# Attention's keys: weighted and turned by VectorE in 32x32 blocks and laid out through device memory, in place of the transposes on TensorE

## The chip, the cores and the metric

The kernel runs on one core of one Trainium2 chip. The metric is the device time of one execution in microseconds. A core has TensorE (PE in the profile, with its weight loads as PEld), VectorE (DVE), ScalarE (ACT), GpSimd (POOL) and SyncE (SP), whose queue issues nearly all DMAs of this kernel. Each engine runs its own instructions in order and waits on semaphores for the others.

## What is computed

The reference is a block of four layers on `x` (16 batches, 64 tokens, 512 wide) with a context of the same shape. The change touches the first layer only, grouped-query attention over context and latents, 32 query heads on 8 key heads of 128:

```python
kv = concat([context, layernorm(x)], axis=1)         # 128 keys for each batch
q = rms_norm((layernorm(x) @ Wq) heads) * q_norm_w   # 32 heads
k = rms_norm((kv @ Wk) heads) * k_norm_w             # 8 heads
v = (kv @ Wv) heads
scores = einsum('bhgqd,bhkd->bhgqk', q, k) / sqrt(128)
x = x + (softmax(scores) @ v) heads @ Wo
```

Behind it come a feed-forward layer with weights quantized to 4 bits, an attention without projections, and a feed-forward layer with low-rank parts. All is in float32; the large products are made as three products of high and low parts.

## The kernel before

Attention is cut into 64 units: key head g (8 of them) by pair of batches p (8). `run_steps` runs `*_step0` for each step j on every engine, and a unit passes through the stages with a lag: in step j the kernel projects queries and keys of unit j, makes the scores of unit j-1, the softmax of unit j-2, the product with the values of unit j-3 and the output projection of unit j-4. `st.has(lag, UNITS)` says whether a stage has a unit in this step.

PE's order in a full step is written out in `pe_step0`: the query projection (L439, 12 products of 512 columns), the key and value projection (L459, 24 of 256), the two key transposes of unit j-1 (L485), the output projection of unit j-4 (L505, 12 of 512), the values (L526), the scores of unit j-1 (L469). In step 3 the scores of unit 2 come right behind the transposes, ahead of the values.

The queries already go another way than the keys. DVE scales them (L711) from PSUM bank `b_q` into bank `b_n`, in an order in which each 32x32 block can be turned by itself, and turns the blocks (L717) into `qB`. SP writes `qB` to `q_turn` in device memory (`blocks_out`, L372) and reads it back as `qT` (`blocks_back`, L376). The probabilities take the same way (L691, L696, `p_turn`, `pR`). The read of unit j's queries waits until the scores of unit j-1 are done, since `qT` is a single buffer.

The keys: ACT sums their squares (L632, squares into `ksq`), DVE makes the mean (L720), POOL the power -0.5 (L808), DVE the scaled keys `kn` (L723), PE two transposes into bank 2 (L485), ACT a copy to `kT` that multiplies by the product of both norm weights (L626, one number for each partition, `wqk[:, 3:4]`). DVE then adds the output projection into `acc` (L740), and its next step begins with the row maximum of the scores (L674) and the low part of the values (L678), for which the key projection two units later waits (`s_vlo`).

SP's queue in `sp_step0`: probabilities out, weight pieces, stores of dequantized weights, queries out, probabilities back, loads for the dequantization, queries back. In step 0 the loads of the last quantization table and of four index lists (`sp_tables(sp, (2,))`, `sp_indices`, L887 to L902) stand behind the queries' read.

## Time and profile before

| what | value |
|---|---|
| median of 3 runs | 1081.14 us (1079.81 to 1081.6) |
| the profiled execution | 1080.24 us, span 1078.4 us |
| PE busy | 1038.6 us (96%) |
| DVE busy | 711.7 us (66%) |
| ACT busy | 536.8 us (50%) |
| POOL busy | 469.5 us (44%) |
| mean granted TensorE clock | 0.995 of full speed |
| attention's steps | to about 700 us of the span |

Busy time is the time in which an engine executes; matmuls overlap in the pipeline, so starts tell more than durations. The span is what the profile covers; the run's own time is 1.8 us longer.

### The profile page before, as it was taken

The numbers are of one execution on the slowest core, as the hardware profiler recorded it, in microseconds if no ns is written. First come the engines' busy times: TensorE is split into PE (matmuls) and PEld (weight loads), VectorE is DVE, ScalarE is ACT, GpSimd is POOL, SyncE is SP. The second block draws the span as 40 slices with busy tenths as digits, with TensorE's granted clock in tenths as the row PEclk, the third lists the DMA queues.
The fourth block names the chain that finished last, engine by engine and source line by source line (L and its number), as shares of the span: only waits on it lengthen the run. The fifth ranks groups of instructions, "written<-read, shape, count | busy, mean of one in ns | idle before, by whom it ended". The sixth has DMA issues, their size and how long they took to land. (4 is left out here: it accounts for less than half of the span.)

```text
span 1078.4 us, 18680 instructions
## 1 busy us (share of the span) xinstructions
PE 1038.6 (96%) x6021; PEld 897.1 (83%) x6021; DVE 711.7 (66%) x1435; ACT 536.8 (50%) x1974; POOL 469.5 (44%) x446
## 2 busy tenths in 40 slices
PE   5899999999999999999999999899999999899998
PEld 5789999999899899899999998778777877677877
DVE  6677767667666667667676666653345666889862
ACT  3555555555555555555555454433324445456531
POOL 3445454565554554554645433300013325566521
PEclk9999999999999999999999999999999999899999
DMA  8447766676667666766666435242021344233301
GB/s 284 112 130 226 207 192 198 195 206 196 199 198 195 201 192 186 214 204 201 210 191 187 145 99 167 98 136 82 1 59 40 79 108 108 69 69 69 89 11 40
DMA packets 151397, 156.18 MB, mean 145 GB/s; under 512 B 19640, under 2 KB 104656, under 8 KB 151300
## 3 DMA queue, kind: packets, MB, share of 16 engines
q1 hardware_dynamic: 146804, 138.08, 44.0%
q0 software_dynamic: 4496, 16.91, 5.3%
q8 instruction: 49, 0.80, 0.3%
q14 instruction: 48, 0.39, 0.1%
HBM read 98.19 MB, written 44.30 MB: 132 GB/s over the span
## 5 line engine op out<-in xcount | busy, mean ns | idle before, releaser
L459 PEld LDWEIGHTS bank<-wqkv,kvT 128*128 128x128 f32 x1536 | 193.9, 193 | 8.2 <-issue 3.6
L439 PE MATMUL bank<-wqkv,kvT 128*128 128x512 f32 x768 | 195.4, 404 | 5.0 <-DVE wqkv L746 2.5
L459 PE MATMUL bank<-wqkv,kvT 128*128 128x256 f32 x1536 | 196.2, 285 | 3.0 <-issue 3.0
L800 POOL TENSOR_TENSOR rms<-msq,half_neg 128x4 f32<-128x4 f32 x64 | 79.5, 1242 | 270.0 <-DVE msq L703 270.0
L505 PE MATMUL bank<-wo,aoT 128*128 128x512 f32 x768 | 190.7, 398 | 0.3 <-DVE aoT L659 0.3
L439 PEld LDWEIGHTS bank<-wqkv,kvT 128*128 128x128 f32 x768 | 141.2, 191 | 34.1 <-issue 3.2
L505 PEld LDWEIGHTS bank<-wo,aoT 128*128 128x128 f32 x768 | 139.8, 189 | 26.4 <-DVE aoT L659 0.5
L606 ACT ACTIVATE prob<-bank,nmax 128x128 f32<-128x128 f32 x256 | 90.4, 365 | 56.4 <-DVE nmax L674 56.4
L646 ACT ACTIVATE aoT<-bank 128x512 fp32r<-128x512 f32 x64 | 38.2, 597 | 121.7 <-PE bank L526 96.2
L803 POOL TENSOR_TENSOR pT<-pR,pT 128x512 fp32r<-128x512 f32 x64 | 82.3, 1286 | 14.4 <-ACT pT L595 14.4
L613 ACT ACTIVATE qB<-bank 128x128 f32<-128x128 f32 x256 | 67.3, 278 | 39.7 <-PE bank L439 36.2
L711 DVE TENSOR_TENSOR bank<-bank,rms 128x512 f32<-128x512 f32 x64 | 44.8, 699 | 55.8 <-POOL rms L800 55.8
L1054 PE MATMUL bank<-x2T,wgu 128*128 128x512 f32 (+1 forms) x336 | 80.9, 396 | 0.4 <-DVE wgu L1015 0.4
L2125 POOL TENSOR_TENSOR pr<-pr,rc 128x512 f32<-128x512 f32 x52 | 54.4, 1048 | 54.5 <-DVE rc L1989 54.3
L674 DVE TENSOR_REDUCE nmax<-bank 128x4 f32<-128x512 f32 x64 | 44.2, 691 | 50.1 <-PE bank L469 50.0
L1054 PEld LDWEIGHTS bank<-x2T,wgu 128*128 128x128 f32 (+1 forms) x336 | 62.4, 187 | 15.9 <-DVE wgu L1015 0.8
L626 ACT ACTIVATE kT<-bank,wqk 128x256 f32<-128x256 f32 x64 | 30.6, 478 | 87.9 <-PE bank L485 87.9
L469 PE MATMUL bank<-kT,qT 128*128 128x128 f32 x512 | 67.8, 275 | 2.0 <-DMA qT<-q_turn 1.3
L1073 PE MATMUL bank<-wd,hT 128*128 128x512 f32 (+1 forms) x264 | 65.5, 396 | 0.0
L469 PEld LDWEIGHTS bank<-kT,qT 128*128 128x128 f32 x512 | 62.8, 192 | 2.5 <-DMA qT<-q_turn 1.5
L723 DVE TENSOR_TENSOR kn<-bank,rms 128x256 f32<-128x256 f32 x64 | 27.2, 425 | 52.0 <-POOL rms L808 52.0
L1869 ACT ACTIVATE pmT<-bank 128x512 fp32r<-128x512 f32 x64 | 38.2, 596 | 46.4 <-PE bank L1588 46.2
(176 smaller groups left out, 2021.4 us busy)
## 6 DMA issues: line engine op xcount, KB each, us to landing
q_turn<-qB SPq DMA_DIRECT2D x64, 256.0 KB
qT<-q_turn SPq DMA_DIRECT2D x64, 256.0 KB, 3.6
p_turn<-pB SPq DMA_DIRECT2D x64, 256.0 KB, 2.1
pR<-p_turn SPq DMA_DIRECT2D x64, 256.0 KB
qS<-qhl SPq DMA_DIRECT2D x32, 256.0 KB, 3.7
wqkv_raw<-in_L_xattn_Wq_dram SPq DMA_DIRECT2D x30, 256.0 KB
wo_raw<-in_L_xattn_Wo_dram SPq DMA_DIRECT2D x30, 256.0 KB
wload<-w_gu SPq DMA_DIRECT2D x20, 256.0 KB, 3.2
```

The lines of the kernel that those rows point to most:

```text
L439: mm = pe.matmul(b_q[:, :], kvT[:, l, kt, p, 1:3, :], wqkv[:, par, r, kt, 0:QW], start=(kt == 0 and n == 0), stop=(kt == KT - 1 and n == 2))
L459: mm = pe.matmul(kv_bank(st, 0)[:, b * 256:(b + 1) * 256], kvT[:, l, kt, p, 2 * b:2 * b + 2, :], wqkv[:, par, r, kt, QW:QKV], start=(kt == ...
L469: mm = pe.matmul(b_s[:, n * P:(n + 1) * P], qT[:, n, :, :], kT[:, n // 2, :], start=True, stop=True)
L505: mm = pe.matmul(b_o[:, :], aoT[:, l, h, :, :], wo[:, par, r, h, :], start=(h == 0 and n == 0), stop=(h == G - 1 and n == 2))
L606: act.activation(prob[:, :, n, :], b_s[:, n * P:(n + 1) * P].rearrange("p (k b) -> p b k", b=4), ACT.Exp, bias=nmax[:, n:n + 1], accum_out ...
L613: act.activation(qB[:, h, :, :], b_q[:, h * HD:(h + 1) * HD], ACT.Square, accum_out=ssq[:, h:h + 1]).then_inc(s_qsq, 1)
L711: dve.tensor_tensor(b_n[:, :].rearrange("p (b h d) -> p b h d", b=4, h=G), b_q[:, :].rearrange("p (h d b) -> p b h d", h=G, b=4), rms[:, 0 ...
L800: pool.tensor_tensor(rms[:, 0:4], msq[:, 0:4], half_neg[:, 0:4], ALU.pow).then_inc(s_rq, 1)
L803: pool.tensor_tensor(pT[:, LO, :, :, :], pR[:, :, :, :], pT[:, HI, :, :, :].bitcast(F32), ALU.subtract).then_inc(s_plo, 1)
L1054: mm = pe.matmul(b[0:w, :], wgu[:, f, l, m, kt, 0:w], x2T[:, r, kt, :], start=(kt == 0 and k == 0), stop=(kt == KT - 1 and k == 2))
L1073: mm = pe.matmul(f_d[t][:, :], hT[0:w, l, t * P:(t + 1) * P], wd[0:w, f, r, :], start=(f == 0 and k == 0), stop=(f == FT - 1 and k == 2))
L2125: pool.tensor_tensor(of[:, to + t % KT, :], of[:, to + t % KT, :], rc1[:, t % 4:t % 4 + 1].to_broadcast([P, D]), ALU.mult).then_inc(s_n1, 1)
```

## The change

The keys take the queries' way. DVE multiplies the keys of each batch by their norm factor and by the norm weights (now a row of 128 numbers on every partition, loaded with a broadcast) in one `scalar_tensor_tensor` for each of the two batches, from the projection's bank into `b_n`, turns the blocks into `kB`, and SP writes `kB` to `k_turn` and reads it back as `kT`. PE's two transposes and ACT's copy are gone, and `kn` and `ksq` with them: ACT writes the squares into bank 2 (`b_sq`). The cut diff:

```diff
-        kn = sb("kn", [P, 2, HD], F32, s0b)
+        kB = sb("kB", [P, G, 2, 32], F32, s0b)
-        kT = sb("kT", [P, 2, P], F32, s0b)
+        kT = sb("kT", [P, G, 2, 32], F32, s0b)
+        wqk = sb("wqk", [P, 2, HD], F32, s0b)
...
+        k_turn = nc.dram_tensor("k_turn", (G, P, 2 * 32), F32).ap()
...
-            sp.dma_start(wqk[:, 0:1], a["L0_xattn_q_norm_w"].rearrange("(d o) -> d o", o=1)).then_inc(s_nw, 16)
+            sp.dma_start(wqk[:, 0, :], a["L0_xattn_q_norm_w"].rearrange("(o d) -> o d", o=1)
+                         .to_broadcast([P, HD])).then_inc(s_nw, 16)
...
             def sp_step0(st):
+                if st.has(1, UNITS):
+                    sp.wait_ge(s_k_out, st.done(1, 16))
+                    wait(sp, s_s, st.done(2))
+                    blocks_back(sp, kT[:, :, :, :], k_turn).then_inc(s_k_back, 16)
                 if st.has(2, UNITS):
...
                 sp_loads(sp, st.j)
                 if st.has(0, UNITS):
+                    sp.wait_ge(s_kB, st.done(0))
+                    wait(sp, s_k_back, st.done(1, 16))
+                    blocks_out(sp, k_turn, kB[:, :, :, :]).then_inc(s_k_out, 16)
                     sp.wait_ge(s_q_out, st.done(0, 16))
                     wait(sp, s_s, st.done(1))
                     blocks_back(sp, qT[:, :, :, :], q_turn).then_inc(s_q_back, 16)
...
-            pe.wait_ge(s_kT, st.done(1))
+            pe.wait_ge(s_k_back, st.done(1, 16))
...
-                mm = pe.matmul(b_s[:, n * P:(n + 1) * P], qT[:, n, :, :], kT[:, n // 2, :], start=True, stop=True)
+                mm = pe.matmul(b_s[:, n * P:(n + 1) * P], qT[:, n, :, :], kT[:, :, n // 2, :], start=True, stop=True)
...
-            if st.has(1, UNITS):
-                pe.wait_ge(s_kn, st.done(1))
-                wait(pe, s_kT, st.done(2))
-                for b in range(2):
-                    mm = pe.transpose(turn_bank(st)[:, b * P:(b + 1) * P], kn[:, b, :], ident[:, :])
-                mm.then_inc(s_tk, 1)
...
-                act.activation(kT[:, :, :], turn_bank(st)[:, 0:256].rearrange("p (b k) -> p b k", b=2), ACT.Copy,
-                               scale=wqk[:, 3:4]).then_inc(s_kT, 1)
...
-                    act.activation(ksq[:, b, :], by_key(kv_bank(st, 0))[:, b, 0:HD], ACT.Square,
+                    act.activation(b_sq[:, b * HD:(b + 1) * HD], by_key(kv_bank(st, 0))[:, b, 0:HD], ACT.Square,
...
                 dve.wait_ge(s_rk, st.done(0))
-                wait(dve, s_tk, st.done(1))
-                dve.tensor_tensor(kn[:, :, :], by_key(kv_bank(st, 0))[:, :, 0:HD],
-                                  rms[:, 4:6].unsqueeze(2).to_broadcast([P, 2, HD]), ALU.mult).then_inc(s_kn, 1)
+                if st.j == 0:
+                    dve.wait_ge(s_idx_n, 2)
+                for b in range(2):
+                    mul = dve.scalar_tensor_tensor(
+                        out=b_n[:, 0:256].rearrange("p (a b d) -> p b a d", a=4, b=2)[:, b, :, :],
+                        in0=by_key(kv_bank(st, 0))[:, b, 0:HD].rearrange("p (d a) -> p a d", a=4),
+                        scalar=rms[:, 4 + b:5 + b], in1=wqk[:, 1, :].rearrange("p (d a) -> p a d", a=4),
+                        op0=ALU.mult, op1=ALU.mult)
+                mul.then_inc(s_kn, 1)
+                dve.wait_ge(s_kn, st.done(0))
+                wait(dve, s_k_out, st.done(1, 16))
+                dve.transpose(kB[:, :, :, :].rearrange("p a b t -> p (a b t)"), b_n[:, 0:256]).then_inc(s_kB, 1)
...
-            dve.tensor_tensor(wqk[:, 2:3], wqk[:, 0:1], wqk[:, 1:2], ALU.mult).then_inc(s_idx_n, 1)
+            dve.tensor_tensor(wqk[:, 0, :], wqk[:, 0, :], wqk[:, 1, :], ALU.mult).then_inc(s_idx_n, 1)
```

## Rows read from the trace of the kernel before

**Rows 1.** The page's busy time of each engine over the whole span.

```profile
PE 1038.6 (96%) x6021; PEld 897.1 (83%) x6021; DVE 711.7 (66%) x1435; ACT 536.8 (50%) x1974; POOL 469.5 (44%) x446
```

**Rows 2.** Windows: stretch, length, PE PEld DVE ACT POOL busy us, clock, DMA share, GB/s.

```profile
40.00:60.00 20.00, 14.73 (x95) 12.65 (x95) 16.76 (x40) 11.30 (x49) 9.36 (x10) 0.99 0.44 138
...
300.00:500.00 200.00, 200.00 (x1251) 180.44 (x1250) 137.23 (x275) 110.92 (x490) 107.34 (x92) 1.00 0.68 201
```

**Rows 3.** Timeline of PE, one attention step (start us, duration us, engine, line).

```profile
303.58 3.01 PE L439 MATMUL bank<-wqkv,kvT 128*128 128x512 f32 x12
...
306.43 3.04 PE L459 MATMUL bank<-wqkv,kvT 128*128 128x256 f32 x24
...
309.30 0.38 PE L485 MATMUL bank<-ident,kn 128*128 128x128 f32 x2
...
309.44 2.98 PE L505 MATMUL bank<-wo,aoT 128*128 128x512 f32 x12
...
312.25 0.88 PE L526 MATMUL bank<-pT,vv 128*128 128x256 f32 x6
...
312.97 1.06 PE L469 MATMUL bank<-kT,qT 128*128 128x128 f32 x8
...
313.78 3.01 PE L439 MATMUL bank<-wqkv,kvT 128*128 128x512 f32 x12
```

**Rows 4.** Timeline of DVE around the turn of one attention step.

```profile
301.53 0.42 DVE L723 TENSOR_TENSOR kn<-bank,rms 128x256 f32<-128x256 f32 x1 [0.81 <-POOL rms L808]
...
302.26 0.69 DVE L740 TENSOR_TENSOR acc<-bank,acc 128x512 f32<-128x512 f32 x1 [0.30 <-PE bank L505]
...
303.86 0.69 DVE L674 TENSOR_REDUCE nmax<-bank 128x4 f32<-128x512 f32 x1 [0.91 <-PE bank L469]
...
304.47 0.41 DVE L678 TENSOR_TENSOR vv<-bank,vv 128x256 fp32r<-128x256 f32 x1
```

**Rows 5.** Groups by line and shape, 20 to 830 us: xcount, busy us, mean ns.

```profile
L717 DVE STREAM_TRANSPOSE qB<-bank 128x512 f32<-128x512 f32 x64 | 45.9, 717 | 2.2
...
L711 DVE TENSOR_TENSOR bank<-bank,rms 128x512 f32<-128x512 f32 x64 | 44.8, 699 | 55.8 <-POOL rms L800 55.8
...
L485 PE MATMUL bank<-ident,kn 128*128 128x128 f32 x128 | 24.4, 273 | 0.0
...
L1274 DVE SCALAR_TENSOR_TENSOR gact<-gact,bank 128x512 f32<-128x512 f32 x5 | 3.4, 687 | 5.9 <-ACT gact L1166 5.9
```

**Rows 6.** The page's DMA queue (packets, MB, share) and one issue group (us to landing).

```profile
q1 hardware_dynamic: 146804, 138.08, 44.0%
...
p_turn<-pB SPq DMA_DIRECT2D x64, 256.0 KB, 2.1
```

**Rows 7.** Timeline of SP's DMA issues in start-up, steps 0 and 1.

```profile
28.54 0.39 SPq L376 DMA_DIRECT2D qT<-q_turn  x1
...
31.97 0.64 SPq L902 DMA_DIRECT2D idx_raw<-in_L_ffn_down_g_idx_dram  x1
...
33.20 0.35 SPq L372 DMA_DIRECT2D q_turn<-qB  x1
...
36.45 0.38 SPq L376 DMA_DIRECT2D qT<-q_turn  x1
```

**Rows 8.** Timeline of PE in start-up: first scores, then key projections of units 2 to 4.

```profile
31.33 1.16 PE L469 MATMUL bank<-kT,qT 128*128 128x128 f32 x8 [1.26 <-DMA qT<-q_turn]
...
35.87 3.11 PE L459 MATMUL bank<-wqkv,kvT 128*128 128x256 f32 x24 [0.61 <-issue]
...
47.41 3.11 PE L459 MATMUL bank<-wqkv,kvT 128*128 128x256 f32 x24 [2.37 <-issue]
...
59.14 4.61 PE L459 MATMUL bank<-wqkv,kvT 128*128 128x256 f32 x24
```

**Rows 9.** Windows view: one microsecond of start-up, columns as in rows 2.

```profile
61.00:62.00 1.00, 1.00 (x6) 1.00 (x6) 1.00 (x2) 0.74 (x2) 0.96 (x1) 0.50 0.22 80
```

**Rows 10.** Timeline of DVE in start-up: the maximum of unit 1's scores.

```profile
46.28 0.69 DVE L674 TENSOR_REDUCE nmax<-bank 128x4 f32<-128x512 f32 x1
```

More of the change, by code:

```diff
@@ L107, in block_kernel @@
         rstd = sb("rstd", [P, 4, PAIRS], F32)
-        wqk = sb("wqk", [P, 4], F32)
         s0 = ExitStack()
@@ L125, in block_kernel @@
         qB = sb("qB", [P, G, G, 32], F32, s0b)
-        ksq = sb("ksq", [P, 2, HD], F32, s0b)
         pB = sb("pB", [P, G, G, 32], F32, s0b)
-        kn = sb("kn", [P, 2, HD], F32, s0b)
+        kB = sb("kB", [P, G, 2, 32], F32, s0b)
         qT = sb("qT", [P, G, G, 32], F32, s0b)
-        kT = sb("kT", [P, 2, P], F32, s0b)
+        kT = sb("kT", [P, G, 2, 32], F32, s0b)
         vv = sb("vv", [P, 2, 2, 2, HD], F32R, s0b)
+        wqk = sb("wqk", [P, 2, HD], F32, s0b)
         prob = sb("prob", [P, 4, 4, 32], F32, s0b)
@@ L236, in block_kernel @@
         s_q, s_kv, s_s, s_pv, s_o = (sem(f"s_{n}") for n in ("q", "kv", "s", "pv", "o"))
-        s_qsq, s_ksq, s_kT, s_vhi, s_exp, s_phi, s_aohi = (
-            sem(f"s_{n}") for n in ("qsq", "ksq", "kT", "vhi", "exp", "phi", "aohi"))
+        s_qsq, s_ksq, s_vhi, s_exp, s_phi, s_aohi = (
+            sem(f"s_{n}") for n in ("qsq", "ksq", "vhi", "exp", "phi", "aohi"))
         s_qms, s_kms, s_qn, s_kn, s_vlo, s_max, s_plo, s_pn, s_aolo, s_acc = (
             sem(f"s_{n}") for n in ("qms", "kms", "qn", "kn", "vlo", "max", "plo", "pn", "aolo", "acc"))
-        s_qB, s_tk, s_pB = sem("s_qB"), sem("s_tk"), sem("s_pB")
-        s_q_out, s_p_out = sem("s_q_out"), sem("s_p_out")
-        s_q_back, s_p_back = sem("s_q_back"), sem("s_p_back")
+        s_qB, s_kB, s_pB = sem("s_qB"), sem("s_kB"), sem("s_pB")
+        s_q_out, s_k_out, s_p_out = sem("s_q_out"), sem("s_k_out"), sem("s_p_out")
+        s_q_back, s_k_back, s_p_back = sem("s_q_back"), sem("s_k_back"), sem("s_p_back")
         s_rq, s_rk = sem("s_rq"), sem("s_rk")
@@ L247, in block_kernel @@
         b_kv = (bank[3], bank[1])
-        b_n = bank[5]
+        b_sq, b_n = bank[2], bank[5]
+        k_turn = nc.dram_tensor("k_turn", (G, P, 2 * 32), F32).ap()
         q_turn = nc.dram_tensor("q_turn", (G, P, P), F32).ap()
@@ L252, in block_kernel @@
         STEPS0 = UNITS + 4
-        def turn_bank(st):
-            return bank[2] if st.j < UNITS else b_q
         def unit(st, lag):
@@ L325, in sp_first @@
             context(2)
-            sp.dma_start(wqk[:, 0:1], a["L0_xattn_q_norm_w"].rearrange("(d o) -> d o", o=1)).then_inc(s_nw, 16)
-            sp.dma_start(wqk[:, 1:2], a["L0_xattn_k_norm_w"].rearrange("(d o) -> d o", o=1)).then_inc(s_nw, 16)
+            sp.dma_start(wqk[:, 0, :], a["L0_xattn_q_norm_w"].rearrange("(o d) -> o d", o=1)
+                         .to_broadcast([P, HD])).then_inc(s_nw, 16)
+            sp.dma_start(wqk[:, 1, :], a["L0_xattn_k_norm_w"].rearrange("(o d) -> o d", o=1)
+                         .to_broadcast([P, HD])).then_inc(s_nw, 16)
             latents(3)
@@ L621, in act_step0 @@
                 x2_hi(act, 1)
-            if st.has(1, UNITS):
-                act.wait_ge(s_tk, st.done(1))
-                if st.j == 1:
-                    act.wait_ge(s_idx_n, 2)
-                act.activation(kT[:, :, :], turn_bank(st)[:, 0:256].rearrange("p (b k) -> p b k", b=2), ACT.Copy,
-                               scale=wqk[:, 3:4]).then_inc(s_kT, 1)
             if st.has(0, UNITS):
@@ L758, in dve_first @@
             dve.wait_ge(s_nw, 32)
-            dve.tensor_tensor(wqk[:, 2:3], wqk[:, 0:1], wqk[:, 1:2], ALU.mult).then_inc(s_idx_n, 1)
+            dve.tensor_tensor(wqk[:, 0, :], wqk[:, 0, :], wqk[:, 1, :], ALU.mult).then_inc(s_idx_n, 1)
             dve.wait_ge(s_idx_n, 1)
-            dve.tensor_scalar(wqk[:, 3:4], wqk[:, 2:3], float(HD) ** -0.5, None, ALU.mult).then_inc(s_idx_n, 1)
+            dve.tensor_scalar(wqk[:, 1, :], wqk[:, 0, :], float(HD) ** -0.5, None, ALU.mult).then_inc(s_idx_n, 1)
             dve_statistics(dve, 2)
```

## The prediction

> **What bounds the kernel now.** I read the page's busy times first: PE works 96% of the span, DVE 66% [rows 1]. Then the windows by stretch: from 300 to 500 us PE is busy for all 200 us, in start-up (40 to 60 us) for only 14.73 of 20, and there DVE is busy for 16.76 [rows 2]. So two regimes stand side by side: a steady one that PE sets, from about 60 us to 671 us, and a start-up that something else sets. PE's timeline shows the steady step as a closed ring: query projection at 303.58, key projection 306.43, transposes 309.30, output projection 309.44, values 312.25, scores 312.97, the next query projection 313.78, with no idle time noted anywhere [rows 3]. The period is 10.20 us. What DVE does in that step is the other thing to see: it waits 0.30 us for the output projection before L740 and 0.91 us for the scores before L674 [rows 4]. DVE is late for nobody and has 1.2 us of rest in a step at this point.
>
> **The change, part by part.** *The transposes on PE.* A record of L485 lasts 273 ns [rows 5], but that is pipeline depth. What a pair costs is start to start: from 309.30 to 309.44, 0.14 us [rows 3]. The queue of PE is full, so the slot is given back if nothing new makes PE wait. Bounds: 0.10 us, if the first product of L505 needs a little more room right behind L459; 0.19 us, if half of the pair's record of 0.38 us [rows 3] stood clear of its neighbours. I take 0.14, as the starts are what the period is made of. Steps 4 to 63 are ones in which PE is the bound or becomes it: 60 x 0.14 = 8.4 us (6.0 to 11.4).
>
> *ACT's copy.* One ACT instruction of a step goes; ACT is half idle, and the only reader of its time here is the sum of squares, which DVE reads behind its own transpose L717. Nothing gained, nothing lost; the squares' new home in PSUM costs ACT nothing that anyone waits for.
>
> *DVE.* Out goes L723, 0.42 us [rows 4]. In come two multiplies of 128 elements and one block transpose of 256. From 512 elements at 0.69 us (L740) and 256 at 0.42 [rows 4] one element costs 1.05 ns and the fixed part is 0.15 us, so 128 elements take 0.29 us; the form with two operations costs what the plain one does (L1274, 687 ns for 512), and reading every fourth element does not either (L711, 699 ns) [rows 5]. A transpose of 512 takes 717 [rows 5], so one of 256 some 0.45. Neighbours on DVE overlap by about 0.08 us (303.86 + 0.69 against a start at 304.47 [rows 4]), which gives 0.21 + 0.29 + 0.45 + 0.03 for the wait between them = 0.98 us, 0.56 more than before; bounds 0.45 and 0.90 (each multiply as dear as the one of 256). Where does it go? L723 ends at 301.95; the new work would end at 302.51, L740 starts 0.25 us late and ends at 303.20, and the scores are there at 303.86, or 303.72 with the shorter step. So 0.5 us of the rest remain, the addition is covered. Even uncovered, the next cover is at L459: the low part of the values is done at 304.88, and PE asks for it at 306.43, 1.55 us later [rows 3, 4].
>
> *SP and DMA in the steady step.* SP gets two waits and two issues. The write of unit j is queued behind the loads and ahead of the queries' read, which waits for the scores (303.86) anyway; `kB` is there at 302.5, so SP waits no longer than before. The read heads the next step: it waits for the write's landing (2.1 us, as `p_turn` [rows 6]), so it is issued at about 305 and lands 2.8 to 3.6 us later, at 309; the scores come at 312.97 [rows 3]. Cover: 4 us. The probabilities' write queued behind it is ready at 307.8 only. The bytes: 128 packets of 1 KB and 512 of 256 B in a step. All packets of the queue took 44% of 16 engines' time for 146804 of them [rows 6], 52 ns each; 640 more are 2.1 us on each of 16 engines in a step, and the DMA share of 0.68 [rows 2] goes to at most 0.88. That costs latency, which the 4 us cover.
>
> The Trainium skill (DMA: Bandwidth & Descriptors, section "Why small descriptors are slow") puts the overhead of a packet of 256 bytes at 27%. No row here splits a packet's time, so nothing can be said for or against it; by that figure the 512 small packets would be the dearest part of the addition, inside the ceiling of 0.88 above.
>
> *Start-up.* Here is the price. In step 0 SP issues the queries' read at 28.54, then the last table and four index lists until 32.61, and only then step 1 begins [rows 7]. The keys' read is now the first entry of step 1, behind all of them. PE waited until 31.33 for `qT` [rows 8], 2.8 us after its issue. The keys' read, issued at 32.65, lands at 35.5 by that, or at 35.9 by the 3.2 us that the write of 33.20 took behind the index lists (the next read goes at 36.45, as it waits for that landing) [rows 7]. I take 35.9: unit 0's scores come 4.6 us late, after almost 6 us of idle PE. What a rest does to the clock: 24 products of the key projection take 3.11 us at 35.87 and 47.41, and 4.61 us at 59.14, behind two rests of some 2 us each; the granted clock there was 0.50 of full speed, the level of 1.2 GHz [rows 8, 9]. So behind the longer rest I expect the half clock, +0.8 us on the scores and about 1.5 us on the query projection behind it. DVE then takes unit 0's maximum at 37.6 in place of 34.75 (it was busy with other work until then), +2.9. The query projection of unit 2 ends 2 us later still than that order gives, of which 1.3 us reaches DVE through the squares; the key work of unit 2 adds 0.56. So unit 1's maximum, at 46.28 before [rows 10], comes at 51.0. From there to unit 4's key projection (59.14 [rows 8]) DVE is the bound (16.76 of 20 us busy [rows 2]) and adds the 0.56 of unit 3: +5.3 us in all, rounded to 5.2. The keys' reads of units 1 and 2 come in time by this order (unit 2's lands at 53.5, its scores start at 54.9). Bounds: 2.4 us, with a landing after 2.5 us, no fall of the clock and 1.1 us of DVE; 8.3 us, with a landing 0.7 us later and the fall of 1.5 us paid once more.
>
> The norm weights as rows make two DVE operations of 128 elements out of two of one (0.29 against the fixed 0.15 us each), ahead of step 0; DVE waits for unit 0's queries behind them, so that covers them, and without the cover it is 0.3 us.
>
> *The end.* In step 64 there is no projection, and PE waits for DVE's work on the next layer while unit 63's queries land; the keys' read follows theirs within 0.4 us. No cost. The layers behind attention are untouched.
>
> *Sum.* The profiled execution took 1078.4 us and 1.8 around it. 1080.2 - 8.4 + 5.2 = 1077.0. The median of the runs lies 0.9 above the profiled one, so 1077.9.
>
> **The rivals.** *A cheap start.* If the half clock does not set in, or its fall at 59 us goes away, start-up costs 2.4: 1081.1 - 8.4 + 2.4 = 1075.1. For it: the clock stayed full behind the rest of 2.37 us at 47.41 [rows 8]. Against: the new rest is more than twice as long. Chance 0.18.
>
> *A dear start.* 8.3 us: 1081.0, no change. For it: the index lists are in the queue ahead of the read, and every later step of start-up has a rest too. Chance 0.14.
>
> *DVE becomes the bound (the slower side).* DVE's ring is 10.20 - 0.91 - 0.30 = 8.99 us now; with 0.56 it is 9.55 against PE's 10.06. It decides from an addition of 1.07 us on. If reads that are strided on both inputs, or `b_n` used three times in a step with waits between, bring it to 1.3, the period is 8.99 + 1.3 = 10.29 and the time 1081.1 + 60 x 0.09 + 5.2 = 1091.7. For it: three more passes each step on the engine that sets start-up. Against: the rows show neither surcharge [rows 5]. Chance 0.07.
>
> The Trainium skill (VectorE: DVE Perf Modes, section "Rules for kernel authors") speaks against this change: it gives a 128x128 transpose to TensorE where the result may lie in PSUM, and to VectorE only blocks of 32x32. The trace so far disagrees for this kernel, since the pair costs the full engine 0.14 us and the exchange costs 0.56 us on the one with rest; by the rule the time would be that of this rival.
>
> *The slot is not given back.* Nothing gained, start-up paid: 1081.1 + 5.2 = 1086.3. For it: only that ends of matmuls are modelled. Against: the starts add up to the period. Chance 0.05.
>
> *The keys' read comes late each step.* DMA share near 0.9 and landings over 7 us; each us beyond the cover is 60 us. Chance 0.02, for 1100 and more.
>
> **How the numbers follow.** The forecast, 1077.9, has 0.54; its own range is 1076.0 to 1079.5. The range over all, with no more than 2 in 10 left out, is 1073.5 to 1083.5. A measurement of this kernel can tell about 0.2% (2.2 us) from no change, so faster means below 1079.0: 0.18 from the cheap start and 0.42 of the forecast, 0.60. Within 0.2%: 0.12 of the forecast and 0.11 of the dear start, 0.23. Slower: the rest, 0.17.
>
> **What would show it.** In PE's timeline of after: L505 at 0.02 us or less where L485 stood, and a period of 10.06 us (right) or 10.2 (slot or DVE). No idle before the scores in steady steps. DVE's wait for the scores at 0.3 to 0.5 us. In start-up: the first scores at 36 us with an idle of 6 us released by the DMA `kT`, the granted clock at half behind it, unit 1's maximum at 51 us. I am wrong if the keys' read lands elsewhere in SP's queue, or if steady steps show a wait for `kT` or for `vv`.

## The result

The change makes the kernel slower: 1094.76 us (median of 4 runs, 1091.59 to 1099.81) against 1080.47 for the kernel before on the same chips; ratio 1.0131, 95% interval 1.0108 to 1.0154. The forecast was 1077.9, the range ended at 1083.5. The profiled execution took 1094.41 us with a span of 1092.6, 14.2 more than the span of before.

The first look is at the busy times, and at the windows of start-up and of the steady part (columns as in [rows 2]), of the changed kernel:

```profile
PE 1031.1 (94%) x5893; PEld 882.9 (81%) x5893; DVE 757.4 (69%) x1563; ACT 514.8 (47%) x1910; POOL 470.3 (43%) x446
```

```profile
40.00:60.00 20.00, 17.05 (x112) 15.27 (x111) 14.63 (x36) 10.68 (x46) 8.82 (x9) 0.95 0.45 137
300.00:500.00 200.00, 195.74 (x1203) 173.93 (x1202) 149.26 (x310) 103.17 (x473) 103.95 (x89) 1.00 0.76 220
```

Against [rows 1]: PE is busy for 7.5 us less, VectorE for 45.7 more. Against [rows 2]: PE was busy for all of 300 to 500 us and now rests 4.3 us of them. VectorE, with 149 us of 200, is not full. Something new makes PE wait in the steady part.

PE's timeline of after shows a step that nothing disturbs, and further on one that is disturbed (columns as in [rows 3]; a bracket is the idle time before the instruction):

```profile
308.05 1.06 PE L476 MATMUL bank<-kT,qT 128*128 128x128 f32 x8
308.86 3.01 PE L446 MATMUL bank<-wqkv,kvT 128*128 128x512 f32 x12
311.71 3.04 PE L466 MATMUL bank<-wqkv,kvT 128*128 128x256 f32 x24
314.58 2.91 PE L506 MATMUL bank<-wo,aoT 128*128 128x512 f32 x12
317.33 0.88 PE L527 MATMUL bank<-pT,vv 128*128 128x256 f32 x6
...
324.57 2.91 PE L506 MATMUL bank<-wo,aoT 128*128 128x512 f32 x12
...
548.26 1.13 PE L476 MATMUL bank<-kT,qT 128*128 128x128 f32 x8 [1.94 <-issue]
```

The output projection starts at 314.58 and 324.57: a period of 9.99 us in place of 10.20 [rows 3]. So the slot of the transposes is given back, and it was worth 0.21 us, not 0.14. The gain is eaten by other steps. Setting the start of the output projection of each step beside that of the kernel before gives this account of the two spans (+ is later):

| stretch | us |
|---|---|
| start-up, to step 4 | +3.65 |
| 59 steps by 0.205 from step 4 to step 63 | -12.1 |
| step 6, stalled | +2.9 |
| steps 7 to 62, stalls in 20 of them, the longest 2.2 us | +15.6 |
| steps 64 and 65, where the next layer sets in | +3.2 |
| later | +1.0 |
| sum | +14.2 |

The account sets one execution beside one other. Executions of kernels whose code is the same there differ by up to some 3 us in start-up and by some 2 us in steps 64 and 65 (shown below), so the first and the last rows are less certain than the steady ones.

The stalls of the steady part are the item to explain. What SP waited for between 80 and 640 us of after (engine and line, what for, us in total, times, longest):

```profile
SPq L383 <- DMA k_turn<-kB: 153.7, 53, 7.1
SPq L918 <- DMA w_gu<-qch: 41.4, 24, 2.4
...
SPq L379 <- DVE pB L691: 7.8, 7, 2.9
```

and of before:

```profile
SPq L372 <- DVE pB L696: 172.8, 55, 3.6
...
SPq L914 <- DMA w_gu<-qch: 13.9, 19, 2.2
```

Before, SP stood at the head of each step waiting for the probabilities: it was early. Now it stands there waiting for the keys' write to land, and the probabilities stand ready behind it. SP's own timeline in after has the whole ring:

```profile
304.98 0.37 SPq L383 DMA_DIRECT2D kT<-k_turn  x1
305.47 0.43 SPq L379 DMA_DIRECT2D p_turn<-pB  x1
...
307.59 0.41 SPq L930 DMA_DIRECT2D w_gu<-qch  x1
...
311.42 0.56 SPq L918 DMA_DIRECT2D qch<-in_L_ffn_up_qweight_dram  x1
312.06 0.54 SPq L379 DMA_DIRECT2D k_turn<-kB  x1
312.70 0.39 SPq L383 DMA_DIRECT2D qT<-q_turn  x1
314.96 0.37 SPq L383 DMA_DIRECT2D kT<-k_turn  x1
315.43 0.46 SPq L379 DMA_DIRECT2D p_turn<-pB  x1
```

and VectorE's timeline of after beside it says when the data of these transfers were ready:

```profile
308.28 0.45 DVE L728 STREAM_TRANSPOSE kB<-bank 128x256 f32<-128x256 f32 x1
...
309.23 0.67 DVE L669 TENSOR_REDUCE nmax<-bank 128x4 f32<-128x512 f32 x1
...
312.43 0.72 DVE L691 STREAM_TRANSPOSE pB<-bank 128x512 f32<-128x512 f32 x1
...
318.41 0.80 DVE L720 SCALAR_TENSOR_TENSOR bank<-bank,rms,wqk 128x128 f32<-128x128 f32 x2 [0.81 <-POOL rms L812]
319.24 0.45 DVE L728 STREAM_TRANSPOSE kB<-bank 128x256 f32<-128x256 f32 x1
```

The keys' read goes out at 304.98, the probabilities' write behind it at 305.47, then the store of dequantized weights (307.59); the load at 311.42 waits for that store's landing; the keys' write stands behind the load and goes out at 312.06, 3.3 us after `kB` was complete (308.73); and the next keys' read (314.96) stands behind the write's landing. `pB` was complete at 313.15 and goes out at 315.43, 2.3 us late. All that SP waits for in this round are landings of its own transfers, and from read to read it takes 9.98 us, as long as PE's step, so nothing is left over. That equality belongs to this round only: the stores and loads differ from step to step, and the twelve rounds whose read goes out between 294 and 409 us last 8.81 to 12.77 us. What tells most is how long the probabilities lie ready before their write goes out, in the median of the steps between 95 and 640 us: 0.03 us in the kernel before, 2.2 us here. A store or a write that lands late then moves what is behind it: the probabilities reach PE late (L527 waits 7.8 us in 10 steps between 80 and 640 us), or the keys seem to (L476, 4.6 us in 9 steps, such as the 1.94 us above; the profile names no releaser there, but the keys' read had gone out at 545.94 only, 2.3 us before the scores).

Start-up is the other item. SP, after:

```profile
29.01 0.38 SPq L383 DMA_DIRECT2D qT<-q_turn  x1
...
32.42 0.64 SPq L906 DMA_DIRECT2D idx_raw<-in_L_ffn_down_g_idx_dram  x1
33.10 0.43 SPq L383 DMA_DIRECT2D kT<-k_turn  x1
```

and PE, after:

```profile
36.09 2.05 PE L476 MATMUL bank<-kT,qT 128*128 128x128 f32 x8 [6.54 <-DMA kT<-k_turn]
37.78 4.89 PE L446 MATMUL bank<-wqkv,kvT 128*128 128x512 f32 x12
```

The read behind the index lists, PE idle for 6.5 us, the scores and the query projection at half speed (2.05 us against 1.06, 4.89 against 3.01; the granted clock of 36 to 41 us was 0.50 of full speed, the level of 1.2 GHz): that is what was forecast.

### The profile page after: what moved, and what is told of

Read it like the earlier page. It is cut to its first block and busy times, and to the rows that moved or that the text cites. A ratio compares the mean times of both kernels' runs of the same rounds, so it can differ in the third digit from the quotient of the medians.

```text
span 1092.6 us, 18679 instructions
## 1 busy us (share of the span) xinstructions
PE 1031.1 (94%) x5893; PEld 882.9 (81%) x5893; DVE 757.4 (69%) x1563; ACT 514.8 (47%) x1910; POOL 470.3 (43%) x446
## 5 line engine op out<-in xcount | busy, mean ns | idle before, releaser
L506 PE MATMUL bank<-wo,aoT 128*128 128x512 f32 x768 | 186.4, 391 | 1.4 <-DVE aoT L654 1.4
L506 PEld LDWEIGHTS bank<-wo,aoT 128*128 128x128 f32 x768 | 140.3, 188 | 28.2 <-DVE aoT L654 1.5
L720 DVE SCALAR_TENSOR_TENSOR bank<-bank,rms,wqk 128x128 f32<-128x128 f32 x128 | 51.1, 446 | 52.1 <-POOL rms L812 52.1
L476 PE MATMUL bank<-kT,qT 128*128 128x128 f32 x512 | 69.9, 280 | 11.1 <-DMA kT<-k_turn 6.5
L476 PEld LDWEIGHTS bank<-kT,qT 128*128 128x128 f32 x512 | 64.1, 195 | 13.1 <-issue 12.3
L527 PEld LDWEIGHTS bank<-pT,vv 128*128 128x128 f32 x384 | 53.3, 190 | 19.3 <-POOL pT L807 15.4
L527 PE MATMUL bank<-pT,vv 128*128 128x256 f32 x384 | 57.6, 286 | 9.5 <-POOL pT L807 9.2
L1873 ACT ACTIVATE pmT<-bank 128x512 fp32r<-128x512 f32 x64 | 38.2, 597 | 46.1 <-PE bank L1592 45.7
```

The source lines that it names most:

```text
L476: mm = pe.matmul(b_s[:, n * P:(n + 1) * P], qT[:, n, :, :], kT[:, :, n // 2, :], start=True, stop=True)
L506: mm = pe.matmul(b_o[:, :], aoT[:, l, h, :, :], wo[:, par, r, h, :], start=(h == 0 and n == 0), stop=(h == G - 1 and n == 2))
L527: mm = pe.matmul(b_pv[:, b * 256:(b + 1) * 256], vv[:, par, l, b, :], pT[:, r, :, b, :], start=(n == 0), stop=(n == 2))
```

## Experiments: each part alone, on the kernel before

The theory after the result: the wait at the head of SP's queue costs the time; traffic, VectorE's work and the missing transposes do not. Rivals: the DMA engines are overloaded by 640 more packets in a step, or VectorE's longer chain delays PE.

**No transposes.** The kernel before without the two transposes; ACT copies `kn`, and the keys enter the scores unturned.

```diff
-                for b in range(2):
-                    mm = pe.transpose(turn_bank(st)[:, b * P:(b + 1) * P], kn[:, b, :], ident[:, :])
-                mm.then_inc(s_tk, 1)
...
-                act.activation(kT[:, :, :], turn_bank(st)[:, 0:256].rearrange("p (b k) -> p b k", b=2), ACT.Copy,
+                act.activation(kT[:, :, :], kn[:, :, :], ACT.Copy,
```

> The kernel before without the two key transposes on PE, and with nothing in their place: ACT copies the keys from kn without turning them, so the scores are not the reference's. It measures the slot alone. In the undisturbed steps of the changed kernel the period is 9.99 us against 10.20, so 0.21 us a step and not the 0.14 of the forecast: 60 x 0.21 = 12.6 us, 1068 us. If the forecast's 0.14 were right and the rest of the 0.21 came from elsewhere (ACT, the other order), 1072 us. If the slot were not given back, 1080.

Measured: 1070.24 us, ratio 0.990 (0.9881 to 0.992). The period is 9.99 us, so the slot is 0.21 us, and the whole of it is worth 9.6 us. It is less than 60 x 0.21 because of places where PE does not set the pace: step 6 takes 13.0 us here, against 10.20 in the kernel before, and the last steps take 1.5 us more; start-up came 1.5 us earlier in this execution. In step 6 VectorE of this kernel waits for the first load of quantized weights:

```profile
83.84 0.49 DVE L1205 TENSOR_SCALAR qch<-qch,shift 128x512 int32<-128x512 int32 x1 [4.58 <-DMA qch<-_L_ffn_gate_qweight_dram]
```

No keys travel in this kernel, so that stall does not need them.

**The traffic alone.** The kernel before, and in each step a write of 128 KB from `kvT` to a spare array and a read of it back in the same shapes as the keys' (of the edit only the read is shown). The read waits for the write of the step before last, which has long landed.

```diff
+                if st.has(2, UNITS):
+                    sp.wait_ge(s_k_out, st.done(2, 16))
+                    wait(sp, s_k_back, st.done(3, 16))
+                    blocks_back(sp, kY[:, :, :, :], k_turn[st.j % 2]).then_inc(s_k_back, 16)
```

> The kernel before with the added DMA traffic alone: at the changed kernel's places in SP's queue 128 KB is written to device memory and 128 KB read back in each step, from and to tiles that nobody waits for, through two buffers, so that the read at the head of a step waits for the write of the step before last. The squares lie in PSUM to make room. Theory Q (SP's queue: the read at the head of a step waits for the landing of the write issued just before, and holds the probabilities' write and all behind it): no wait, so at most 2 us more than before, 1080 to 1083. Rival C (contention: more packets make every landing later): the 18.7 us of stalls return, 1095 or more. In either case the landings tell by how much traffic alone lengthens them.

Measured: 1081.07 us, ratio 1.0004 (0.9992 to 1.0016). Window of 300 to 500 us:

```profile
300.00:500.00 200.00, 200.00 (x1254) 180.37 (x1253) 137.36 (x274) 111.81 (x488) 108.39 (x93) 1.00 0.77 225
```

The DMA share is 0.77, as in after (0.76), PE does not rest, and the probabilities' write still goes out 0.03 us after its data are ready. Overload falls as the cause.

**The same traffic, and the wait.** One thing differs from the kernel above: the read at the head of the step waits for the write of the step just before.

```diff
-                if st.has(2, UNITS):
-                    sp.wait_ge(s_k_out, st.done(2, 16))
-                    wait(sp, s_k_back, st.done(3, 16))
-                    blocks_back(sp, kY[:, :, :, :], k_turn[st.j % 2]).then_inc(s_k_back, 16)
+                if st.has(1, UNITS):
+                    sp.wait_ge(s_k_out, st.done(1, 16))
+                    wait(sp, s_k_back, st.done(2, 16))
+                    blocks_back(sp, kY[:, :, :, :], k_turn[(st.j - 1) % 2]).then_inc(s_k_back, 16)
```

> The kernel before with the same unused traffic as b2_traffic and one difference: the read at the head of a step waits for the landing of the write issued in the step just before it, as in the changed kernel. PE, DVE and ACT have the old work. Theory Q (the wait at the head of SP's queue is enough to cause the steady stalls): 1090 or more. If the stalls need the key data itself (PE waiting for kT) or the added DVE work, 1080 to 1083 as b2_traffic.

Measured: 1089.23 us, ratio 1.0072 (1.0046 to 1.0098). Its window and what SP waited for:

```profile
300.00:500.00 200.00, 195.23 (x1218) 174.48 (x1217) 135.71 (x266) 108.11 (x475) 103.00 (x89) 1.00 0.75 218
```

```profile
SPq L389 <- DMA k_turn<-kvT: 147.0, 53, 5.3
```

PE rests 4.8 us in this stretch, as in after (4.3), though no result of these transfers is used by anyone. The profiled execution collects 8.9 us of stalls in steps 7 to 62. They can only come through what is queued behind the wait on SP. The probabilities lie ready for 2.2 us in the median, as in after. This is the clearest of the runs: by the two ratios the wait by itself costs about 7 us, the bytes nothing that can be told from zero. It makes 8.9 of the 15.6 us of stalls of after. The others come only where PE also needs the keys and VectorE has the new work; no run parts these two, but the next section shows that nearly all of them go when the read changes its place.

**VectorE's work.** The kernel before, and the two multiplies once more on VectorE, into the bank `b_n`.

```diff
+                for b in range(2):
+                    mul = dve.scalar_tensor_tensor(
+                        out=b_n[:, 0:256].rearrange("p (a b d) -> p b a d", a=4, b=2)[:, b, :, :],
+                        in0=by_key(kv_bank(st, 0))[:, b, 0:HD].rearrange("p (d a) -> p a d", a=4),
+                        scalar=rms[:, 4 + b:5 + b], in1=ident[:, :].rearrange("p (d a) -> p a d", a=4),
+                        op0=ALU.mult, op1=ALU.mult)
```

> The kernel before with the two new multiplies of DVE added behind the scaling of the keys (0.80 us a step, as much as the change adds to DVE in all, 0.86), their result unused. Theory Q: the steady steps cover it, start-up pays two or three times 0.8, so 1080.5 + 0 to 2.5. Rival D (DVE becomes the bound in the steady steps): 1090 or more.

Measured: 1082.46 us, ratio 1.0019 (1.0008 to 1.0029). In the profiled execution steps 7 to 63 gain and lose nothing; step 4 starts 1.0 us later, step 6 takes 0.3 us more and the last steps 2.3. So 0.8 us more of VectorE in each step is covered in the steady part, as forecast. That the multiplies are what costs the rest is not shown: the last steps take 2.0 us more with the traffic alone, too, where VectorE has no new work.

Two further looks say what a multiply costs. With both inputs read plainly, and then with only the one in SBUF read plainly and the one in PSUM in steps of four as before:

> b3_dve_multiplies with both inputs of the added multiplies read in plain order (elements next to each other), the output still in blocks of 32; for the duration of one multiply alone. If the stride of the inputs is what makes it 443 ns in place of the 290 of the forecast, about 290; if it is the operation with a number for each partition and a second tensor, 440 still.

> b3_dve_multiplies with the weights alone (the input in SBUF) read in plain order, the keys from PSUM still every fourth element. If the stride in SBUF costs the time, about 290 ns; if the stride in PSUM does, 440.

The group of L728 in the three kernels, in this order (group, busy us and mean ns of one, idle before):

```profile
L728 DVE SCALAR_TENSOR_TENSOR bank<-bank,rms,ident 128x128 f32<-128x128 f32 x128 | 50.8, 443 | 0.0
```

```profile
L728 DVE SCALAR_TENSOR_TENSOR bank<-bank,rms,ident 128x128 f32<-128x128 f32 x128 | 39.0, 350 | 0.0
```

```profile
L728 DVE SCALAR_TENSOR_TENSOR bank<-bank,rms,ident 128x128 f32<-128x128 f32 x128 | 38.9, 350 | 0.0
```

One execution each (1083.5 and 1081.36 us) tells nothing of the whole time, but the groups are clear: 93 ns of the 443 are the strided read from SBUF, the strided read from PSUM is free, and the form itself takes 350, not the 290 that I had worked out.

## Experiments: moves in SP's queue, on the changed kernel

**The keys' read behind the probabilities' write.** The same instructions, one of them elsewhere:

```diff
             def sp_step0(st):
-                if st.has(1, UNITS):
-                    sp.wait_ge(s_k_out, st.done(1, 16))
-                    wait(sp, s_s, st.done(2))
-                    blocks_back(sp, kT[:, :, :, :], k_turn).then_inc(s_k_back, 16)
                 if st.has(2, UNITS):
...
                     blocks_out(sp, p_turn, pB[:, :, :, :]).then_inc(s_p_out, 16)
+                if st.has(1, UNITS):
+                    sp.wait_ge(s_k_out, st.done(1, 16))
+                    wait(sp, s_s, st.done(2))
+                    blocks_back(sp, kT[:, :, :, :], k_turn).then_inc(s_k_back, 16)
```

> The changed kernel with one move in SP's order: the keys' read stands behind the probabilities' write and no longer ahead of it. Theory Q: the probabilities' write goes when it is ready, the waits of PE for their low part (9.2 us) and of ACT for the probabilities go; what remains is held back with the rest of the queue, so 1084 to 1090. Rivals C and D: no change, 1093 to 1097.

Measured: 1082.6 us, ratio 1.0027 (1.001 to 1.0043): 11.5 of the 14.3 us above the kernel before are gone, more than expected. PE is busy for all 200 us from 300 to 500 again, the stalls of steps 7 to 62 fall from 15.6 to 1.7 us, and SP is early again:

```profile
SPq L379 <- DVE pB L691: 127.5, 49, 3.5
...
SPq L383 <- DMA k_turn<-kB: 25.2, 23, 2.5
```

The read still waits for its write, but 23 times and behind the probabilities, and SP's rest before them (3.5 us at most) takes up what a late store costs. The probabilities' write goes out 0.03 us after its data are ready, as in the kernel before, although the rounds from read to read still last 8.0 to 12.1 us: what counts is what is queued behind the wait.

**The keys' write ahead of the loads.** The read stays at the head.

```diff
-                sp_loads(sp, st.j)
                 if st.has(0, UNITS):
...
                     blocks_out(sp, k_turn, kB[:, :, :, :]).then_inc(s_k_out, 16)
+                sp_loads(sp, st.j)
+                if st.has(0, UNITS):
```

> The changed kernel with the other move alone: the keys' write stands ahead of the dequantization's load (which waits for a store to land) and no longer behind it; the read stays at the head of the step. Theory Q: the write goes when the keys are ready, 2 to 3 us earlier in two steps of three, so its landing is over by the time the probabilities are ready and most steady stalls go: 1083 to 1088. If the stalls come from the read's place alone, no change: 1093 to 1097.

Measured: 1084.95 us, ratio 1.0032 (1.0011 to 1.0052). Stalls of 2.3 us are left in steps 7 to 62. So either cut opens the ring: the landing of the store is the link that this one takes out, and the probabilities' write is what the other frees. But step 6 now takes 6.9 us beyond its 9.99.

**The last table and the index lists behind unit 0's keys' read**, in step 1 in place of step 0, the steady order as in after:

```diff
                     blocks_back(sp, kT[:, :, :, :], k_turn).then_inc(s_k_back, 16)
+                if st.j == 1:
+                    sp_tables(sp, (2,))
+                    sp_indices(sp)
...
-                if st.j == 0:
-                    sp_tables(sp, (2,))
-                    sp_indices(sp)
```

> The changed kernel with the last table and the four index lists issued behind unit 0's keys' read, in step 1. In the profile of the changed kernel PE waited 6.5 us for that read and its clock fell behind it. Theory: the read is issued at 29.4 and lands at 32.5, so 3 us less at the first output projection, 1091 to 1092; the steady stalls stay.

Measured: 1088.1 us, ratio 1.0084 (1.0051 to 1.0117). Step 4 starts 0.95 us later than before in place of 3.65, so by this pair the lists cost 2.7 us of start-up. The other profiled executions agree in direction: the four kernels with the lists ahead of the keys' read start step 4 3.65 to 4.8 us later than the kernel before, the five with the lists behind it from 0.8 us earlier to 2.7 us later. The steady stalls remain (14.1 us), and step 6 hardly stalls (0.3 us beyond 9.99). The time is some 3 us below what was expected.

**Moves together.** First all three, where the lists stand at the head of step 1 and so still ahead of the keys' read; then the read and the lists, with the lists really behind the read; then all three with the lists behind.

> The changed kernel with all three moves in SP's order: the keys' read behind the probabilities' write, the keys' write ahead of the dequantization's load, the tables behind unit 0's keys' read. Theory Q: 60 steps of 9.99 us, start-up 1 to 2 us late by DVE's added work (b3_dve_multiplies lost 1.3 us by the first output projections and 2.3 us in steps 64 and 65), the end 2 to 3.5 us late: 1079.8 - 12.4 + 1.5 + 3 = 1072 (1070 to 1075), faster than both kernels.

> The changed kernel with two moves in SP's order: the keys' read behind the probabilities' write, and the last table and the index lists behind unit 0's keys' read (in a4_all they stood ahead of it after all, in step 1). Theory: a1_read_behind_p lost 4.3 us by the first output projection and 4.3 in step 6 (there DVE waits for the first dequantization loads, which the late start pushes back); with the lists behind, 1.0 and 0.3 as a3_tables_behind. Steady 59 x 0.21 = 12.4 saved less 2 us of single stalls, 3.5 us lost in steps 64 and 65: 1080 + 1.3 - 10.4 + 3.5 = 1074.5 (1072 to 1077). If step 6 is a matter of the read's place and not of the start, 1078 or more.

> As a5_read_and_tables, and the keys' write ahead of the dequantization's load. Theory: no single stalls in the steady steps (none in a4_all from step 8 to 62), but the first loads of step 5 go up to 1 us later: 1072 to 1076. If the write ahead of the loads is what made step 6 of a4_all so dear (9.2 us), 1078 or more.

| moves | us | ratio, 95% | to step 4 | step 6 | stalls 7 to 62 |
|---|---|---|---|---|---|
| none (after) | 1094.76 | 1.0131 (1.0108 to 1.0154) | +3.65 | +2.9 | 15.6 |
| read | 1082.6 | 1.0027 (1.001 to 1.0043) | +4.3 | +4.5 | 1.7 |
| write | 1084.95 | 1.0032 (1.0011 to 1.0052) | +4.6 | +6.9 | 2.3 |
| lists | 1088.1 | 1.0084 (1.0051 to 1.0117) | +0.95 | +0.3 | 14.1 |
| all, lists ahead of the read | 1085.39 | 1.0032 (1.0012 to 1.0052) | +4.8 | +9.4 | 0 |
| read, lists | 1078.57 | 0.9989 (0.9972 to 1.0007) | +0.9 | +4.0 | 1.5 |
| all, lists behind the read | 1080.25 | 0.9994 (0.998 to 1.0008) | -0.3 | +7.8 | 0 |

(Step 6: what it takes beyond 9.99 us; to step 4: against the kernel before; both in the profiled execution.) All three kernels came out slower than expected, by 4 to 13 us. With all three moves the steady stalls are gone entirely, but what was won there is lost in step 6. I had written that a late start-up pushes step 6 into trouble. The last row refutes it: no late start, and +7.8.

What holds step 6 shows on VectorE, in the kernel with read and lists moved:

```profile
84.02 0.83 DVE L1215 TENSOR_SCALAR qch<-qch,shift 128x512 int32<-128x512 int32 x1 [2.35 <-DMA qch<-_L_ffn_gate_qweight_dram]
...
87.70 1.71 DVE L1219 TENSOR_TENSOR qch<-qch,rows 128x512 f32<-128x512 int32 x1 [1.22 <-DMA rows<-table_gate,idx]
```

and on PE:

```profile
91.25 1.33 PE L476 MATMUL bank<-kT,qT 128*128 128x128 f32 x8 [1.36 <-DMA qT<-q_turn]
```

VectorE's rows are the first two pieces of the dequantization, whose loads SP issues at 80.16, right behind the seven table copies and among the exchanges of queries, keys and probabilities; the DMA share between 80 and 85 us is 0.89, from 85 to 90 it is 1.00. The rest of VectorE's work for attention stands behind these two waits. PE rests as well, but not by that way alone: its longest rest in step 6 of this trace, 1.36 us, stands before the scores, which need both reads. The queries' read, which the profile names, went out at 82.18 and had landed at 90.29; the keys' read went out at 88.01 only, when the keys' write of 81.55 had landed after 6.4 us. So the long landings of the exchange itself hold PE here too. The query projection behind it takes 4.49 us in place of 3.01.

**The two loads and the table copies earlier; weights in plain order.** Three kernels: the weights' row stored in the order in which the multiplies take it; with it the two loads and the seven copies of step 5 issued at the end of step 4; and this last move on the kernel before. (The copies and the two loads leave their places in step 5; those deletions are not shown.) The first two stand on top of the read and the lists moved.

```diff
-                        scalar=rms[:, 4 + b:5 + b], in1=wqk[:, 1, :].rearrange("p (d a) -> p a d", a=4),
+                        scalar=rms[:, 4 + b:5 + b], in1=wqk[:, 1, :].rearrange("p (a d) -> p a d", a=4),
...
-            dve.tensor_scalar(wqk[:, 1, :], wqk[:, 0, :], float(HD) ** -0.5, None, ALU.mult).then_inc(s_idx_n, 1)
+            dve.tensor_scalar(wqk[:, 1, :].rearrange("p (a d) -> p a d", a=4),
+                              wqk[:, 0, :].rearrange("p (d a) -> p a d", a=4), float(HD) ** -0.5, None, ALU.mult).then_inc(s_idx_n, 1)
```

```diff
                     blocks_back(sp, qT[:, :, :, :], q_turn).then_inc(s_q_back, 16)
+                if st.j == 4:
+                    quantized_load(sp, 0)
+                    quantized_load(sp, 1)
+                    for k, (m, n, g) in enumerate(WEIGHTS):
+                        for b in range(-(-n // D)):
+                            w = min(D, n - b * D)
+                            sp.dma_start(table[k, b][:, 0:w], z_line[k][:, b * D:b * D + w]).then_inc(s_tab, 16)
```

> The kernel with the keys' read behind the probabilities' write and the last tables behind unit 0's keys' read (1078.6, 0.9989 of the kernel before); in addition the norm weights stand in the row in the order in which the multiplies take them, so that the operand in SBUF is read plainly. Theory (PE sets the steady step, DVE only start-up, step 6 and the last steps): each multiply takes 350 ns in place of 443, the steady period stays at 9.99 us, and the time falls by 0.3 to 0.9 us, 1077.9. Rival (DVE sets the time somewhere in steady steps after all): 60 x 0.19 us less, 1067.

> The kernel of c1_plain, and the first two dequantization loads and the seven table copies of step 5 issued at the end of step 4, where SP rests 3.5 us and the DMA share is 0.3 to 0.4. Theory (step 6 stalls since these loads and the exchanges of queries, keys and probabilities meet in a full queue at 80 to 90 us): VectorE's two waits there (2.35 and 1.22 us) go, the stall of 3.75 us at step 7 falls below 1 us, the clock stays full, and the time is 1074.5 (0.995 of before). Rival (the stall comes from the longer work of VectorE there, or the table copies now hold the probabilities' write of step 5): the stall stays at 3 to 4 us, 1078.

> The kernel before with that same move of loads and copies from step 5 to the end of step 4, and nothing else. It shows what the move is worth without the change. Theory: in the kernel before, VectorE's waits at step 6 (0.96 and 0.52 us) do not reach PE (steps there are 10.2 us), so nothing is gained, 1080.5 within 1 us. Rival (it gains as much there as in c2_early): 1077.

Measured: plain order 1074.87 us, ratio 0.9941 (0.9916 to 0.9966); with the early loads 1075.04, ratio 0.9934 (0.9907 to 0.9962); the early loads on the kernel before 1080.01, ratio 0.9994 (0.9977 to 1.0011). With the early loads VectorE has no wait for a load or a gather between 76 and 100 us, step 6 takes 9.99 us, and the clock is full there:

```profile
80.00:90.00 10.00, 10.00 (x63) 8.99 (x62) 6.97 (x15) 5.42 (x24) 6.42 (x7) 1.00 0.88 259
```

against the plain order alone:

```profile
80.00:90.00 10.00, 8.02 (x50) 6.80 (x49) 5.56 (x12) 4.56 (x20) 5.59 (x6) 1.00 0.95 287
```

So with those first loads and gathers early, the stall of step 6 is gone, as expected. This is one execution of each kernel, and loads and copies were moved together; the changed kernel with the lists alone moved lost only 0.3 us in step 6 with the loads in their old place. The lateness of the loads is therefore the likely cause, not one shown beyond doubt. The kernel before had the same meeting with slack to spare, so there the move is worth nothing. What the medians do not show is a gain of the early loads over the plain order (1074.87 against 1075.04, the runs of each spread over 5 to 6 us), although step 6 takes 2.5 us less in the profiled execution. Why stays open: the start-up of the profiled executions differs by 3.4 us (-0.76 and +2.66 us to step 4) although the two kernels are the same up to there, and the plain order's profiled execution, 1078.86, was the slowest of its six. For the same reasons I leave open how much of the 3.7 us between 1078.57 and 1074.87 is the plain order's (it was sized at 0.3 to 0.9, the two stand on different chips, and each multiply did fall to 354 ns). The steady period stayed at 9.99 us, so VectorE does not set it.

Both of these are faster than the kernel before, by 0.6%. The change has something to give; as it stood, the place of one instruction in SP's queue cost it 11.5 us (14.3 us above the kernel before on its chips, against 2.8).

## Why the prediction was wrong, point by point

- **The slot.** Mechanism right: given back, closed ring, bound PE. The term was mis-sized: 0.21 us, not 0.14 (bounds 0.10 to 0.19), 12.1 us and not 8.4. I took the distance of two starts, L485 to L505 [rows 3]; the rest of the pair's price lay behind it: from L505 to L526 it was 2.81 us [rows 3], from L506 to L527 it is 2.75. What shows the price is the period with and without.
- **VectorE.** The block transpose took 0.45 us as forecast, each multiply 446 ns and not 290. From the first start to the last end the new work takes 1.28 us in place of 0.42 (307.45 to 308.73 in the step above), so the addition is 0.86 us and not 0.56, within the upper bound of 0.90. Covered in the steady part, as said; 1.07 us, the point from which this rival decides, was not reached, and its expected sign (a period of 10.29 us) did not come: the loss has another cause. The rule of the Trainium skill that gives whole transposes to TensorE (VectorE: DVE Perf Modes, section "Rules for kernel authors") would have steered clear of this loss, but not for its reason: with the keys' read behind the probabilities' write, the lists moved and the weights in plain order the version without TensorE's transposes is the faster one, by 0.6% (1074.87 us, ratio 0.9941).
- **SP and DMA in the steady step: this is the step that failed.** It said "`kB` is there at 302.5, so SP waits no longer than before", "it waits for the write's landing (2.1 us, as `p_turn`)" and "the probabilities' write queued behind it is ready at 307.8 only". The landing of `k_turn` took 4.5 us in the median (the traffic alone: 3.3), more than twice the row that I had taken. The write did not go out when `kB` was ready but behind a load that waits for a store's landing, which in turn was issued behind the read at the head. I looked at each wait with the others held still; they form a ring through SP, and its sum, 9.98 us in the round shown and up to 12.77 in others, is what had to be set against PE's 9.99. And the cover that I counted, 4 us until the scores, is the keys' own. What stood behind the read, the probabilities' write, had its own deadline, and no cover was worked out for it beyond its being later: it went out a median 2.2 us late, PE waited, and the steady steps lost 15.6 us that the sum put at nothing.
- **Its rival.** "The keys' read comes late each step" had 0.02 and a price of over 1100. It came nearest, but came in 20 steps of 56, not in all, and through the ring, not through the DMA share: 0.76, below the 0.88 allowed for, and at 0.77 harmless in the kernel with the traffic alone.
- **Start-up.** Right in mechanism and near in size: read issued at 33.10 (32.65), scores at 36.09 (35.9), idle 6.54 us (almost 6), half clock on the scores and the query projection, unit 1's maximum at 51.56 (51.0). It came to 3.65 us at step 4 in place of 5.2, in one execution, and with the lists moved 2.7 of them go.
- **Step 6.** Not seen. [rows 2] start their steady stretch at 300 us, and I took steps 4 to 63 as PE's from there. The row that would have told is VectorE's wait for the first load in the kernel before, 0.96 us at 82.04: a place without slack for a shorter step. In the kernel without transposes, where only the step is shorter, that step takes 2.8 us more than before.
- **The end.** "No cost" did not come: 3.2 us in steps 64 and 65. PE rests there for VectorE's work on the next layer. The kernel with read and lists moved, PE:

```profile
675.52 1.77 PE L1107 MATMUL bank<-ident,xn 128*128 128x128 f32 x8 [3.51 <-DVE x2T L1295]
677.09 1.92 PE L476 MATMUL bank<-kT,qT 128*128 128x128 f32 x8
```

and the same place in the kernel before:

```profile
678.92 1.23 PE L1103 MATMUL bank<-ident,xn 128*128 128x128 f32 x8 [2.78 <-DVE x2T L1291]
679.99 1.06 PE L469 MATMUL bank<-kT,qT 128*128 128x128 f32 x8
```

The rest is 0.7 us longer, and behind it both groups run at about half speed (granted clock 0.66 from 675 to 680 us). How much of the 3.2 us is the change's stays open. Its profile is set beside one execution of the kernel before whose clock stayed full there. Kernels with no new work on VectorE lose much of it too, with a granted clock of 0.66 to 0.85 in stretches of 5 us there: 2.0 us with the traffic alone (a rest of 3.14 us, then 1.68 and 1.91 us for the same two groups), 1.5 without transposes (2.98, then 1.94 and 1.74), 1.9 with the early loads on the kernel before (3.09, then 1.23 and 1.50, and 4.24 for the output projection that took 3.00).

- **The sum.** -12.1 for -8.4; +3.65 for +5.2; and +15.6, +2.9, +3.2 and +1.0, four items, for nothing. The first two errors both lie on the fast side, 5.3 us together; step 6, the end and what came later take 7.1 us the other way. So without the ring's stalls the time would have been about 1079 (1094.76 - 15.6), inside the range, and in good part by luck.

## What to carry to other kernels

When an instruction with a wait is put into a queue that issues for several streams, follow the queue round once: add up issue, landing and each wait that stands in it until the same instruction comes again, in each kind of step, and compare that sum with the step. Then ask of everything behind the wait when its data are ready, not only whether the waiting transfer itself has cover. And a step that is made shorter meets its own thin places: look for the small waits of the other engines in the stretches that are not typical (the first load, the last unit), since a gain in the steady part is lost there first.

## What the runs showed of the hardware

- Two 128x128 transposes in a full queue of PE cost 0.21 us together; one record of them says 273 ns [rows 5].
- A `scalar_tensor_tensor` of 128 elements takes 350 ns with plain reads and 443 to 446 with one SBUF operand read in steps of four; the same stride on a PSUM operand adds nothing.
- A write of 128 KB landed after 4.5 us in the median in the changed kernel, with a DMA share of 0.76, and after 3.3 us in the kernel with the traffic alone, with 0.77: the share by itself does not tell the landing. For a stream that nobody waits for, 256 KB of such traffic in each step were free (ratio 1.0004).
- The same start-up code took 3.4 us more or less to step 4 in two kernels' profiled executions. Differences of start-up below that need more than one trace, and steps 64 and 65 took 1.5 to 2.0 us more in three kernels that give VectorE no new work.
